# Two transformer layers with mixtures of experts: routed experts for all tokens, or rows sorted by expert into fixed tiles

## The reference

```python
x = x + L0_attn(layernorm(x))   # 16 heads of 128, rotary, causal; w = sgn * exp(|s| - max|s|), divided by its sum of |.|
x = x + L0_ffn(layernorm(x))
x = x + L1_attn(layernorm(x))   # 16 heads of 16, rotary, softmax
x = x + L1_ffn(layernorm(x))
```

```python
scores = sigmoid(x @ gate_weight.T)
_, sel = top_k(scores + expert_bias, 4)
w = scores[sel] / scores[sel].sum() * scaling
for g, u, d, we in experts:          # we is 0 where the token did not choose the expert
    acc = acc + we[:, None] * (silu(x @ g.T) * (x @ u.T) @ d.T)
out = acc + silu(x @ sg.T) * (x @ su.T) @ sd.T
```

## Time and profile before

| | us |
|---|---|
| median of 3 runs | 938.91 |
| the runs | 934.93, 938.91, 941.91 |
| the profiled execution, its own time | 934.15 |
| its span | 932.1 |
| of it: attention of layer 0, to the last q/k projection | 370.3 |
| end of that attention, beside the first items | 57.3 |
| feed-forward of layer 0 | 150.7 |
| start of attention of layer 1 | 24.3 |
| its steps | 159.6 |
| its end, beside the first items | 27.2 |
| feed-forward of layer 1 | 137.9 |

### The profile page before, as it was taken

One profiled execution on the slowest core, in us unless ns is written; L12 is line 12 of the kernel. 1 busy time (PEld: TensorE's weight loads), 2 busy tenths in 40 slices (PEclk: granted clock), 3 DMA queues, 4 the chain that ended last, 5 costly groups with the idle time before them and its releaser, 6 DMA issues.

```text
span 932.1 us, 14643 instructions
## 1 busy us (share of the span) xinstructions
PE 861.5 (92%) x4476; PEld 654.2 (70%) x4476; DVE 632.5 (68%) x1350; ACT 501.2 (54%) x1093; POOL 430.9 (46%) x361
## 2 busy tenths in 40 slices
PE   3799999999999999799799999698899999899997
PEld 2577777777777777577688778554343357788886
DVE  4778888888888887777645667675578636744543
ACT  2688888888888887743222222104557653322221
POOL 3756665555555566423366763311210122356652
PEclk9899999999999999998999999856889989999999
DMA  4223222223322222112376310441242011333412
GB/s 134 85 91 91 92 90 90 91 91 124 110 92 90 90 90 79 40 58 92 94 212 182 90 46 24 140 166 61 99 133 83 29 35 45 112 101 108 118 46 68
DMA packets 52954, 86.52 MB, mean 93 GB/s; under 512 B 7777, under 2 KB 18529, under 8 KB 52897
## 3 DMA queue, kind: packets, MB, share of 16 engines
q1 hardware_dynamic: 52896, 85.80, 29.5%
HBM read 59.30 MB, written 9.57 MB: 74 GB/s over the span
## 4 chain that ended last, share of the span: by engine, by line
PE 74%; DVE 12%; issue 5%; POOL 3%; DMA 3%; ACT 2%; SPq 1%; POOLq 0%; DVEq 0%; ACTq 0%
PE ps L309 8%; PE ps L837 8%; PE ps L817 8%; PE ps L826 8%; PE ps L320 7%; PE ps L368 6%; PE ps L357 4%; PE ps L331 4%; PE ps L347 3%; PE ps L1309 3%; PE ps L1321 3%; PE ps L1261 3%; PE ps L1240 2%; DVE hid_lo L943 1%; PE ps L375 1%
## 5 line engine op out<-in xcount | busy, mean ns | idle before, releaser
L909 POOL TENSOR_TENSOR guw<-gu,cwb 128x512 f32<-128x512 f32 x64 | 97.6, 1526 | 130.3 <-DVE gu L939 115.7
L868 ACT ACTIVATE gu<-ps 128x512 f32<-128x512 f32 x68 | 40.7, 599 | 187.9 <-PE ps L817 180.4
L939 DVE TENSOR_TENSOR gu<-gu,ps 128x512 f32<-128x512 f32 x64 | 43.9, 685 | 112.5 <-PE ps L826 112.5
L1534 DVE TENSOR_REDUCE nm<-ps 128x1 f32<-128x512 f32 x128 | 81.3, 684 | 30.7 <-PE ps L1261 30.5
L943 DVE TENSOR_TENSOR hid_lo<-guw,hid_hi 128x512 fp32r<-128x512 f32 x68 | 78.4, 1154 | 15.0 <-ACT hid_hi L873 14.9
L1438 ACT ACTIVATE e<-ps 128x512 f32<-128x512 f32 x128 | 68.3, 601 | 35.1 <-PE ps L1309 34.8
L457 DVE TENSOR_TENSOR q_rot<-ps,q_sin 128x512 f32<-128x512 f32 x64 | 44.1, 691 | 61.5 <-POOL q_sin L498 32.6
L837 PE MATMUL ps<-ew_hi,hid_hi 128*128 128x256 f32 x272 | 79.2, 291 | 6.4 <-DVE hid_lo L943 5.8
L893 POOL TENSOR_TENSOR ew_lo<-ew_raw,ew_hi 128x768 fp32r<-128x768 f32 x34 | 71.2, 2093 | 28.9 <-DVE ew_hi L926 28.9
L481 DVE SCALAR_TENSOR_TENSOR w<-ex,rden,sgn 128x512 f32<-128x512 f32 (+3 forms) x128 | 80.9, 691 | 2.9
L498 POOL TENSOR_TENSOR q_sin<-q_sw,sin 128x512 f32<-128x512 f32 x64 | 81.3, 1291 | 0.9 <-DMA q_sw<-q_in 0.7
(11 more groups left out here) (176 smaller groups left out, 2417.2 us busy)
## 6 DMA issues: line engine op xcount, KB each, us to landing
q_sw<-q_in SPq DMA_DIRECT2D x128, 128.0 KB, 2.0
cwb<-cw_dram SPq DMA_DIRECT2D x64, 256.0 KB, 3.4
ew_raw<-in_ew SPq DMA_DIRECT2D x34, 384.0 KB, 4.3
wqk_raw<-in_wqk SPq DMA_DIRECT2D x32, 256.0 KB, 2.7
wv_raw<-in_wv SPq DMA_DIRECT2D x32, 128.0 KB, 2.2
wo_raw<-in_wo SPq DMA_DIRECT2D x32, 128.0 KB, 2.1
qs<-stk_q SPq DMA_DIRECT2D x16, 256.0 KB, 3.7
ks<-stk_k SPq DMA_DIRECT2D x16, 256.0 KB, 4.1
```

The lines of the kernel that those rows point to most:

```text
L909: pool.tensor_tensor(ff[f].guw[:, i % 2, :], ff[f].gu[:, i % 2, :], ff[f].cwb[:, k, :], ALU.mult).then_inc(sem("guw"), 1)
L1534: dve.tensor_reduce(nm1[:, quad % 2, col:col + 1], ps[:, turn_bank("max", n), :], AX.X, ALU.max, negate=True).then_inc(sem("max"), 1)
```

## The change

The routed experts are computed only for rows that chose them. Each token writes its normalised row four times to DRAM (`xs_dram`), at places sorted by expert, each expert's run padded to tiles of 128. The number of tiles is fixed, 3968 / 128 = 31 a half (`TILES_H`), 62 a layer, whatever the counts; a half has 2048 such rows, 16 tiles' worth. Routing therefore also computes `place` (the row number of each choice), with a count of earlier rows from matmuls with a 0/1 matrix (`ranks` on PE), `owner` (the expert of each tile) and `wk` (the four weights).

- **POOL** writes the rows with indirect DMAs, 16 a half (`scatter`), and fetches the results with 16 more (`gather`, in four steps; of the last AHEAD tiles a step need not wait for all). DVE adds them to x with their weights (`combine`, 16 operations a half). `weighted`, the broadcast `cwb` and the split of routed experts' weights are gone.
- **SP** loads a tile (`xg`), PE transposes it (two of 128x128), ACT copies the transposes (`xgT`, 256 columns). PE loads the tile's expert number into a register and addresses the weights with it: two fp32 matmuls of 256 columns give gate and up. ACT takes silu (128 columns), DVE the product (128), PE transposes it, ACT copies that (128), PE has one fp32 matmul of 256 columns for down, DVE copies the result (256), SP stores it. The stages of one tile lie in four turns of the loop.
- The 16 experts' weights of a layer lie in SBUF in fp32 (`exw`, 384 KB each), loaded during attention: two a step in steps H0-5 to H0+2 of layer 0, and in quads 3 to 6 of layer 1.
- `xs_dram` is first filled with zeros, 62 tiles of 128 KB, in the steps that `ZERO_AT` lists.
- The shared expert is left in split form, one item a half.
- LN and logits of half 0 move into step H0+2, the score transposes to N0-5, `ranks` to N0-3, in layer 1 to steps 24 to 30. LN and routing of half 1 stand in half 0's tile loop at `LN_J` to `RANK_J` and `ROUTE_J`, the combination of half 0 in half 1's loop at `COMB_J`, that of layer 0's half 1 in the ramp of layer 1's attention (`COMB_K`), whose q/k groups move later.

The core of the diff; POOL's pieces of attention are as they were, so that a scatter or gather stands in their order:

```diff
+H_SLOTS = (S * TOPK + (P - 1) * E) // P * P
...
+        ZERO_AT = {0: (0, 0, 8), 1: (0, 8, 16), 2: (0, 16, 24), H0 - 5: (0, 24, 28), H0 - 4: (0, 28, 31), H0 - 3: (1, 0, 6),
+                   H0 - 2: (1, 6, 12), H0 - 1: (1, 12, 18), H0: (1, 18, 24), H0 + 1: (1, 24, 31)}
...
+            if i in ZERO_AT:
+                h, first, last = ZERO_AT[i]
+                sp.wait_ge(sem("zeros"), 1)
+                sp.dma_start(xs_dram[h].rearrange("(j p) d -> p j d", p=P)[:, first:last, :],
+                             zeros[:, :].unsqueeze(1).broadcast_to([P, last - first, D])).then_inc(sem("zero_st"), 16)
+            if H0 - 5 <= i <= H0 + 2:
+                for e in range(2):
+                    expert_load(sp, 0, 2 * (i - (H0 - 5)) + e)
...
+            if i == N0 - 4:
+                ew_low(pool, 0)
+            if i == N0 - 3:
+                pool.wait_ge(sem("zero_st"), 16 * len(ZERO_AT))
+                scatter(pool, 0, 0)
...
-            if i == N0 - 3:
-                pe.wait_ge(sem("q_rot"), 2 * N0)
-                ln_pe(pe, 1, (0,))
-            if i == N0 - 2:
-                logits(pe, 0, 0)
-                gate(pe, 0, 0)
-                up(pe, 0, 0)
-            if i == N0 - 1:
-                gate(pe, 0, 1)
-            if i == N0:
-                up(pe, 0, 1)
-                gate(pe, 0, 2)
-                cw_turn(pe, 0, 0)
-                up(pe, 0, 2)
-                gate(pe, 0, 3)
-                up(pe, 0, 3)
-                ln_pe(pe, 1, (1,))
             if i == -1:
                 pe.wait_ge(sem("bo_row"), 1)
                 pe.wait_ge(sem("xT_lo"), 2 * DC)
...
+            if i == H0 + 2:
+                pe.wait_ge(sem("q_rot"), 2 * (i + 3))
+                ln_pe(pe, 1, (0,))
+                logits(pe, 0, 0)
+                pe.wait_ge(sem("score_e"), 1)
+            if i == N0 - 5:
+                pe.wait_ge(sem("q_rot"), 2 * (i + 3))
+                score_turn(pe, 0, 0)
+                pe.wait_ge(sem("score_rd"), 1)
+            if i == N0 - 3:
+                pe.wait_ge(sem("q_rot"), 2 * N0)
+                pe.wait_ge(sem("fixed"), 7)
+                ranks(pe, 0, 0)
+            if i == N0 - 2:
+                pe.wait_ge(sem("place"), 1)
...
+        LN_J, LOGIT_J, SCORE_J, RANK_J = 4, 6, 9, 18
+        ROUTE_J = {9: 1, 11: 1, 13: 1, 18: 1, 19: 1}
+        COMB_J = {8: 0, 11: 1, 14: 2, 17: 3}
+        LN2_STATS_J, LN2_XN_J, LN2_J = 19, 21, 23
+        W1_AT = {4 * part + 2: part for part in range(5)}
+        AHEAD = {3: 3, 2: 2, 1: 1, 0: 0}
+
...
+            placed(0)
+            for n in range(LOAD_AHEAD):
+                load(n)
+            for n in range(NJ):
+                end = (n // TILES_H + 1) * TILES_H
+                if n + LOAD_AHEAD < end:
+                    load(n + LOAD_AHEAD)
                 if f == 0:
...
+                store(n)
+                if n == TILES_H - 3:
+                    placed(1)
+                    for k in range(XG):
+                        load(TILES_H + k)
...
+            def gate_up(n):
+                h, j = divmod(n, TILES_H)
+                if j == 0:
+                    wait_f(pe, f, "owner", h + 1)
+                    wait_f(pe, f, "exw_ld", 16 * E)
+                owner[n] = pe.value_load(r.owner[0:1, h, j:j + 1], min_val=0, max_val=E - 1)
+                wait_f(pe, f, "xt", n + 1)
+                wait_f(pe, f, "h_gu", n - 1)
+                for c in range(DC):
+                    last = pe.matmul(ps[:, HID_BANK[n % 2], 0:2 * P].rearrange("p (a k i) -> p a k i", a=1, k=2),
+                                     r.xgT[:, n % 2, c * P:(c + 1) * P],
+                                     r.exw[:, bass.ds(owner[n], 1), c:2 * DC:DC, :], start=c == 0, stop=c == DC - 1)
+                last.then_inc(sem("h_ps"), 1)
+
+            def turn_h(n):
+                wait_f(pe, f, "h_gu", n + 1)
+                wait_f(pe, f, "ht", n)
+                pe.transpose(ps[:, HT_BANK, 0:P], r.hg[:, n % 2, :], ident[:, :]).then_inc(sem("ht_ps"), 1)
+
+            def down(n):
+                wait_f(pe, f, "ht", n + 1)
+                wait_f(pe, f, "yt", n)
+                pe.matmul(ps[:, YT_BANK, 0:D].rearrange("p (a k i) -> p a k i", a=1, k=2), r.hgT[:, n % 2, :],
+                          r.exw[:, bass.ds(owner.pop(n), 1), 2 * DC:3 * DC, :], start=True, stop=True).then_inc(sem("yt_ps"), 1)
...
+                    gate_up(n)
+                    if j + 2 < TILES_H:
+                        turn_x(n + 2)
+                    if j > 0:
+                        turn_h(n - 1)
+                    if j > 1:
...
+        def scatter(pool, f, h):
+            wait_f(pool, f, "place", h + 1)
+            for t in range(QT):
+                for k in range(TOPK):
+                    pool.indirect_dma_start(xs_dram[h], bass.IndirectOffsetOnAxis(ap=ff[f].place[:, h, t, k:k + 1], axis=0),
+                                            xn[:, h * QT + t, :], None).then_inc(sem(f"place_st{h}"), 16)
...
+        def gather(pool, f, h, step):
...
+            for t in range(QT):
+                pool.indirect_dma_start(ff[f].yg[:, step, t, :], None, ys_dram[h][0:tiles * P, :],
+                                        bass.IndirectOffsetOnAxis(ap=ff[f].place[:, h, t, k:k + 1], axis=0)
+                                        ).then_inc(sem(f"yg_ld{step}"), 16)
...
+            scatter(pool, f, 1)
+            for step in range(TOPK):
+                gather(pool, f, 0, step)
...
+                dve.scalar_tensor_tensor(out=x[:, h * QT + t, :], in0=ff[f].yg[:, step, t, :], scalar=ff[f].wk[:, h, t, k:k + 1],
+                                         in1=x[:, h * QT + t, :], op0=ALU.mult, op1=ALU.add).then_inc(sem("comb"), 1)
...
+            def take_y(n):
+                wait_f(dve, f, "yt_ps", n + 1)
+                wait_f(dve, f, f"ys_st{n % YS}", 16 * (n // YS))
+                dve.tensor_copy(r.ys[:, n % YS, :], ps[:, YT_BANK, 0:D]).then_inc(sem("yt"), 1)
...
+                dve.tensor_scalar(r.place[:, h, :, :], r.top[:, :, 0:TOPK], -1.0, None, ALU.add).then_inc(sem("place"), 1)
...
+                dve.tensor_scalar(r.owner[:, h, 0:TILES_H], r.npast[:, :], float(E - 1), None, ALU.min).then_inc(sem("owner"), 1)
...
-        GROUP_STEP = {-6: (4, 0), -4: (4, 1), -3: (5, 0), -1: (5, 1), 1: (6, 0), 3: (6, 1), 5: (7, 0), 7: (7, 1)}
-        V_STEP = {9: 2, 11: 3}
-        TAIL_Y = TILES // HEADS - LEAD
...
+        GROUP_STEP = {-1: (4, 0), 0: (4, 1), 1: (5, 0), 2: (5, 1), 3: (6, 0), 5: (6, 1), 7: (7, 0), 9: (7, 1)}
...
+        STATS_STEP, XN_STEP, LN_STEP, LOGIT_STEP, SCORE_STEP, RANK_STEP = 24, 25, 26, 27, 28, 30
+        COMB_K = {-6: 0, -5: 1, -4: 2, -3: 3}
+        LN_K = -2
         ZT_TAIL, ZC_TAIL = 7, 3
...
+                if g in (0, 1, 2, 3):
+                    gather(pool, 0, 1, g)
...
+            scatter(pool, 1, 0)
             ln_pool(pool, 3, (1,))
...
+            for step in range(TOPK):
+                combine(dve, 1, 1, step)
...
+            for step in range(TOPK):
+                gather(pool, 1, 1, step)
```

## The result

The changed kernel took 1076.88 us (median of 4 runs, 1066.53 to 1083.02) beside 940.41 for the kernel before (4 runs): a ratio of 1.141, 95% interval 1.128 to 1.154. Slower, as forecast, but by 136 us, not 34, and above the range. Measured again three times (on the chips 12, 7 and 3; the number of the first chip is not on record), the same program took 1017.68, 1017.21 and 1026.14 us; the first of them has a ratio of 1.085 (1.075 to 1.095). So there are two gaps to explain: some 48 us between the forecast 970 and 1018, and 59 us more where it was first measured.

What follows compares the result with a forecast made beforehand. PE was taken as the bound (74% of the chain), chiefly in the routed experts. Three stretches, +10, +8 and +16, made +34 on 934.15, 968, and 970 us as the expected median; range 915 to 1040.

Steps and rivals of the forecast that it cites:

- the forecast column: Whole kernel by stage: the prediction's terms added up, for example 402.3 to layer 0's `place`; sum 966.7 us.
- Arithmetic, and the tile: Routed experts' tile loops: matmuls and transposes 1.60 us, expert number load 0.2, so 1.80 us a tile (1.60 to 2.20).
- One indirect DMA: Scatters and gathers on POOL: each holds POOL for 1.1 us, priced as POOL's pass `wv_lo`; a batch of 16 takes 17.6.
- the 60 that the prediction holds uncovered: Four places on the chain: 16 + 12 + 16 + 16 indirect DMAs uncovered; the sum moves 60 us per us of price.
- The rivals on either side (0.32 and 2.0): Indirect DMA on POOL: cheap, 0.32 us, total 923, chance 0.18; whole transfer, 2.0, total 1024, chance 0.23 (shared with tile 2.2).
- 16 us for what is inserted into layer 0's heads: Layer 0's last heads: LN and logits 5.3, score transposes 1.8, routing about 6, bulk loads about 3; 16 us, rounded.
- The fourth term, 6 for routing on DVE: Layer 0's last heads: DVE's routing pieces inserted ahead of the last ones add about 6 us.
- From the last projection to `place`: End of layer 0's attention: one head, 11.4 us, and 4.6 of small DVE pieces uncovered; 16 us.
- +7 for layer 1's attention: Layer 1, first maximum to last product with v: +4 for the ramp and +3 for moved q/k groups.
- the +4: Ramp of layer 1's attention on DVE: maxima, combine and LN make 31 us against some 27.
- the +3 for the moved groups: Layer 1's attention: q/k groups now inside steps at 1.2 GHz, a pass 0.63 us against 0.39; +3 us.
- the rival on the tile loops: Tile loops: the clock falls to half, a tile goes from 1.6 to 2.6 us, 124 us more, total 1090; chance 0.05.

Runs made afterwards that it cites:

- The repeat: The changed kernel measured again unedited on chip 12, the second measurement: 1017.68 us.
- e1: Changed kernel with half 0's scatter of layer 0 moved on POOL behind the last head's causal selections: 1006.02 us, ratio 1.070.
- e2: Changed kernel with all 128 indirect DMAs replaced by plain ones of the same size on the same queue: 1002.40 us.
- e0: The changed kernel once more, word for word, on chip 12: 1017.68 us, ratio 1.085.
- e4: Changed kernel with layer 0's bulk transfers of weights and zeros spread over the 16 steps inside the two loops: 1006.93 us.
- e8: Kernel before with the changed kernel's places for layer 1's later q/k groups and its SP order around them: 961.59 us, ratio 1.030.
- e10: Changed kernel with the DMAs for quad 3's maxima issued on SP right behind the rows of group 7: 1012.68 us, ratio 1.082.
- e12: Kernel before with the changed kernel's q/k group places, and quad 3's maxima ahead of the wait on SP: 947.25 us, ratio 1.011.
- e5: Changed kernel with a tile's expert number as a constant instead of a register loaded on PE: 1016.21 us.
- e7: Changed kernel with 26 fixed tiles a half instead of 31: 997.53 us.

## Why the prediction was right or wrong

The time lies outside the range. Against the forecast column the first measurement is 104 us longer: 27 to `place`, 30 in layer 1's attention, 46 in the two tile stages. The repeat is 50 us longer: 27, 24 and -4, with small rests. The first two are steps of the prediction that failed, and their causes are shown in part. The third failed in the first measurement alone, and its cause is open.

- **Arithmetic, and the tile: right.** Forecast 1.80 us; measured 1.83 in the rows above, 1.77 as a mean in layer 1. Without the load it is 1.61 to 1.62 (forecast 1.60), so the load costs 0.17 (forecast 0.20). Its own row has a median of 302 ns, of which a part is hidden. The Trainium skill puts the floor of a tensor load at about 600 ns ("DMA: Bandwidth & Descriptors", Latency and other measured facts). If that is this load, the trace is at half of it.
- **One indirect DMA: near.** 1.27 us against 1.1, 10 us over the 60 that the prediction holds uncovered. The rivals on either side (0.32 and 2.0) fall. The price was taken over from another instruction of POOL, and no run ties it to that; its nearness is in part luck. e1 and e2 show that the batch ahead of the selections is on the chain, e2 the batches ahead of layer 1's first tile and in the tail. The spacing is 1.27 us where DVE waits and where it copies tiles from PSUM, with single ones up to 1.7. The "DVE blocks DMA" trap of the Trainium skill ("SBUF — State Buffer", SBUF: two separate sides) is told of an fp32 copy from SBUF to SBUF. None stands beside the batches; the nearest is one cast of 0.62 us (`w_hi<-w_raw`, 556.85 in e0), and the DMA beside it is followed after 1.26 us. So no run here tests it.
- **The step that failed first: 16 us for what is inserted into layer 0's heads.** It is 34 (last q/k at 407.7 against 373.3). LN and logits at H0+1 and H0+2 cost 17 in place of 5.3: I counted the PE's instructions and one wait, and not that `xT_lo` stands behind the head's own DVE work and that the passes behind the wait run at half the clock. The score transposes cost 7 in place of 1.8. The bulk transfers cost 10 in place of 3, which e4 shows; the prediction had named this as a place where its sum could be wrong. The other two are read from the trace. The fourth term, 6 for routing on DVE, has no step of its own among the long ones.
- **From the last projection to `place`: 21.4 us, forecast 13** (its 16 are counted from 370.3, 3 us ahead of the end of that projection). Two runs of routing pieces on DVE stand there, 410.4 to 416.3 and 425.4 to 428.2 in e0, some 8.5 us where 4.6 were taken as uncovered.
- **The step that failed next: +7 for layer 1's attention.** It is +31 in the repeat and +37 in the first measurement. Its two terms came out differently. From the first maximum to the first score, DVE's ramp, it takes 31.0 us against 26.6 before: the +4 is right. From there to the last product with v it takes 159.9 in the repeat and 165.7 first against 133.0: the +3 for the moved groups is +27 and +33. e8 shows 24 for them in the kernel before: 11 to 14 with SP's late maxima, the rest otherwise. The SP queue was not walked at this place, although the change moved group 7 past the maxima on it. In the changed kernel the late maxima explain 4.5 us at most (e10), and what holds its clock down is open. The lengths of a pass that the prediction reads, 0.63 and 0.39 us, are recorded ones and overlap: from start to start a pass takes some 0.42 us at half the clock (278.07 behind 277.66) and 0.23 at full (an item of the earlier trace rows has 36 units of 256 columns in 4.22 us). So half the clock costs nearly twice the time, and the rival on the tile loops (1.6 to 2.6 us) was priced too low.
- **Start of layer 1's attention: 6 us cheaper than forecast, by another path.** 27.7 us against 34.0. The first maximum does not wait for the fourth `rr` behind 12 gathers, but for the rows of the second group behind four (rows at e2).
- **Tiles' stages: the sum right in the repeat**, 273.7 against 277.4, partly by luck. In layer 0 half 0 takes 67.8 us (forecast 73.2), the shared expert 10.2 (9.2), half 1 62.7 (55.8): the stalls of routing were priced too high, and the next LN, which stands in half 1's loop, at nothing there (its tile takes 5.8 us, the one behind it 3.0). Where first measured, it is 49.8 us more than in the repeat by gaps of ACT that no row of before and no other run shows. There the step "ACT has 0.96 us a tile and stays under it" failed, not by ACT's work (53.8 us busy against 53.3 in layer 1's stage) but by its late starts. Their cause is open.
- **The scatter stage and the tail of layer 1: right.** 23.2 and 26.0 us against 23.5 and 23.2. On DVE the tail is four waits for the gathers; two of them:

```profile
1051.32 1.71 DVE L1122 SCALAR_TENSOR_TENSOR x<-yg,wk,x 128x256 f32<-128x256 f32 x4 [5.75 <-DMA yg<-ys_dram,place]
1056.24 1.67 DVE L1122 SCALAR_TENSOR_TENSOR x<-yg,wk,x 128x256 f32<-128x256 f32 x4 [3.21 <-DMA yg<-ys_dram,place]
```

The range reached to 1040 for a dear DMA; the misses lay in steps that had no bound of their own, since I gave the inserted pieces and the moved groups one value each. That the repeat's 1018 lies inside the range is luck: the room was there for the DMA's price, and other steps used it.

## What to carry to other kernels

A fourfold saving in rows was a sixth of PE's time for the experts: fixed tiles were half empty, and 128 rows as a tile take 1.8 us in fp32 with transposes and the load, where they took 1.06 in the split form (4.22 / 4). Against that stand the pieces that routing adds; three of the eight batches of 16 indirect DMAs are shown to stand where little covers them (e1, e2). When work is inserted into a software pipeline of heads, price the wait for the other engine's queue and the passes at half the clock behind it, not the instructions (17 us for 5). When a table moves a step, walk SP's queue past it as well: a small DMA that came 9.6 us late there cost 11 to 14 us (e12).

## What was not expected of the hardware

- The stage of layer 1's attention takes 150 to 180 us in versions whose code there is nearly the same, with a mean clock of 0.87 to 0.65; edits elsewhere of 10 to 20 us can vanish in it (e5, e7, e2). The profiled stages tell more than the total.
- The clock can stay at half while PE is busy nearly all the time: 30.04 of 31.00 us in e12, 37.95 of 40.00 in e8. Both stretches begin while PE works, and not in a wait of several us.
- 16 indirect DMAs hold POOL for 20.3 us, 16 plain ones of the same bytes on the same queue for 8.74.
- In the first measurement this program took 59 us more in the median of its four runs than in the repeat, while the kernel before ran there as elsewhere (940.41). Its trace has ACT starting instructions 2 to 8 us late beside indirect DMAs. The cause is open.
